# Batch norm's folded tables: the mean subtracted behind the products of tokens, tile sums and weights' loads moved into the attention, halves of groups

## The reference, cut to what matters

```python
h = _layernorm(x, axis=-1) * (1 + cb) + sb
q = jnp.einsum('bnd,de->bne', x, w_q)          # x is h here, 2048 columns
mean = jnp.mean(q, axis=(0, 1))
var = jnp.var(q, axis=(0, 1))
q = (q - mean) * jax.lax.rsqrt(var + BN_EPS) * bn_gamma + bn_beta
sim = jnp.einsum('pbnhd,hkpd->pbnhk', q, keys) # 16 groups of 32 keys
...                                            # top 8 of 8, experts, weighted sum
```

## Time and profile before

| | us |
|---|---|
| median of 3 runs (lowest to highest) | 2928.05 (2925.79 to 2930.73) |
| the profiled execution's own time | 2926.95 |
| its span, first to last instruction | 2925.2 |
| TensorE busy | 2720.0 (93%) |
| VectorE busy | 2235.5 (76%) |
| ScalarE busy | 2169.2 (74%) |
| GpSimd busy | 1780.2 (61%) |

### The profile page before, as it was taken

How to read it: one execution, slowest core, us unless ns; L and a number is a source line. 1 busy time by engine, 2 the same in 40 slices (tenths; PEclk the granted TensorE clock), 3 DMA queues, 4 the chain that set the end, 5 groups by cost and what they waited for, 6 DMA issues and landing times. The chain is left out here.

```text
span 2925.2 us, 77676 instructions
## 1 busy us (share of the span) xinstructions
PE 2720.0 (93%) x27972; PEld 2066.3 (71%) x27972; DVE 2235.5 (76%) x8496; ACT 2169.2 (74%) x4273; POOL 1780.2 (61%) x1788
## 2 busy tenths in 40 slices
PE   5999999999999999999999996599999999998588
PEld 3777777777777777777777775366767666766344
DVE  5566866776866776776767755699999999997585
ACT  3888888888888888888888882377767776776574
POOL 3788888888888888888888782234333433432121
PEclk9999999999999999999999997688878878878799
DMA  3000000000000000000000001100000000000000
GB/s 107 1 1 8 1 1 8 1 1 8 1 1 8 1 1 8 1 1 8 1 1 8 1 1 66 69 0 0 0 0 0 0 0 0 0 0 2 1 29 29
DMA packets 11793, 27.63 MB, mean 9 GB/s; under 512 B 1529, under 2 KB 6137, under 8 KB 11137
## 3 DMA queue, kind: packets, MB, share of 16 engines
q1 hardware_dynamic: 11618, 25.48, 2.5%
HBM read 17.07 MB, written 8.40 MB: 9 GB/s over the span
## 5 line engine op out<-in xcount | busy, mean ns | idle before, releaser
L284 POOL TENSOR_TENSOR probs_l<-probs,probs_h 128x512 fp32r<-128x512 f32 x1024 | 1302.7, 1294 | 302.0 <-ACT probs_h L378 297.3
L377 ACT ACTIVATE probs<-bank 128x512 f32<-128x512 f32 x1024 | 641.7, 627 | 266.6 <-PE bank L700 169.6
L539 DVE TENSOR_REDUCE maxes<-ring 128x1 f32<-128x512 f32 x1024 | 659.4, 686 | 181.3 <-PE ring L680 180.4
L378 ACT ACTIVATE probs_h<-bank 128x512 fp32r<-128x512 f32 x1024 | 644.1, 629 | 0.0
L699 PE MATMUL bank<-q_hh,k_hl 128*128 128x512 f32 x1024 | 424.4, 414 | 1.5 <-ACT probs_h L378 1.3
L700 PE MATMUL bank<-q_lm,k_h 65*128 65x512 f32 x1024 | 405.6, 396 | 0.0
L710 PE MATMUL obank<-probs_h,x_l 128*128 128x512 f32 x1024 | 404.7, 395 | 0.0
L712 PE MATMUL obank<-probs_h,x_h 128*128 128x512 f32 x1024 | 403.2, 394 | 0.0
L711 PE MATMUL obank<-probs_l,x_h 128*128 128x512 f32 x1024 | 402.6, 393 | 0.0
L680 PE MATMUL ring<-k_hl,q_hh 128*128 128x512 f32 x1024 | 339.6, 412 | 11.8 <-DVE maxes L539 7.2
L1085 ACT ACTIVATE low_hot<-obank 128x512 f16<-128x512 f32 x512 | 296.8, 604 | 55.3 <-PE obank L1264 42.1
(11 more groups left out here) (255 smaller groups left out, 4827.6 us busy)
## 6 DMA issues: line engine op xcount, KB each, us to landing
xt<-in_x SPq DMA_DIRECT2D x8, 512.0 KB, 10.1
out_x<-xt SPq DMA_DIRECT2D x8, 512.0 KB, 2.6
x<-out_x SPq DMA_DIRECT2D x1, 4096.0 KB, 12.2
out_x<-x SPq DMA_DIRECT2D x16, 256.0 KB, 2.0
mod<-out_x SPq DMA_DIRECT2D x3, 512.0 KB, 13.7
pk_wq<-in_w_q SPq DMA_DIRECT2D x1, 1024.0 KB, 6.1
pk_wqT<-in_w_qT SPq DMA_DIRECT2D x1, 1024.0 KB, 7.3
hot_rule<-in_hot_rule SPq DMA_DIRECT2D x1, 776.0 KB
```

The costliest lines, as they stand in the source:

```text
L284: nc.gpsimd.tensor_tensor(probs_l[:, i, :], probs[:, s % 4, :], probs_h[:, i, :].bitcast(F32), ALU.subtract).then_inc(low_ready, 1)
L377: nc.scalar.activation(probs[:, s % 4, :], st[s % 4], ACT.Exp)
L378: nc.scalar.activation(probs_h[:, i, :], st[s % 4], ACT.Exp).then_inc(st_free[s % 4], 1)
L539: nc.vector.tensor_reduce(maxes[:, i, k:k + 1], ring[bank_of(at)][:], AX.X, ALU.max).then_inc(rows_maxed, 1)
```

## The change

1. **Mean behind the products.** `xt` is no longer changed by the tables: TensorE adds up the products of the tiles as they are, and VectorE takes the outer product of the mean away from them (`outer`, then `cov` in one instruction). The experts subtract the mean where ScalarE copies the transposed tiles (`neg_mean` as bias of `hcT`), and the copy `pk_hT` loses its bias.
2. **Into the attention.** The tile sums of batches 0 to 6 (`tile_sums`, head 5, step 13, one batch later); the loads of the tables' weights, into tiles whose use is over (`spare`, `wmod_sb`), in SyncE's queue before the last batch's stores; the bias's product (`bias_terms` on GpSimd, then one matmul ahead of the last outputs); the products of the first 32 tiles, on TensorE behind its last outputs.
3. **Halves.** The last batch's norm goes by halves of four tiles (`last_moments`, `half_root`, `last_norm`), with a store each. The power, the scaled keys, the matmuls to `w_eff` and the copies go by halves of eight groups.
4. **Bias parts to GpSimd,** with two copies out by ScalarE ahead; `three_ones` too.
5. `hot_rule` gets 128 partitions; the added 31 are zero and never read.

```diff
-            for b in range(B):
+            for b in range(B - 1):
...
+            sp.wait_ge(x1_l_ready, TB * B)
+            for dst, src in table_loads:
+                sp.dma_start(dst, src).then_inc(table_loaded, 16)
+            for half in range(2):
+                tiles = slice((B - 1) * TB + 4 * half, (B - 1) * TB + 4 * half + 4)
+                sp.wait_ge(o_read, 6 * (B * H - 1) + 3 * half + 4)
+                sp.wait_ge(ring_o_read, 2 * (B * H - 1) + half + 2)
+                sp.dma_start(x_scratch[:, tiles, :], xt[:, tiles, :]).then_inc(last_stored[half], 16)
+            sp.wait_ge(table_loaded, 16 * len(table_loads))
...
+            def bias_terms():
+                pool.wait_ge(table_loaded, 16 * len(table_loads))
+                pool.wait_ge(w_ready, B * H + 1)
+                nc.gpsimd.sem_inc(turns, 1)
+                nc.gpsimd.tensor_tensor(bias_of, keysT, spread(scales[:, 1, :], 2, NK), ALU.mult).then_inc(bias_ready, 1)
...
-            root(2 * B)
+            bias_terms()
+            for half in range(2):
+                half_root(half)
...
+            def tile_sums(link, b):
+                dve.wait_ge(h2_ready, 2 * b + 2)
+                batch = xt[:, b * TB:(b + 1) * TB, :].rearrange("p t d -> p d t")
+                link(nc.vector.tensor_reduce((part_sum if b else tile_sum)[:], batch, AX.X, ALU.add))
+                if b:
+                    link(nc.vector.tensor_tensor(tile_sum[:], tile_sum[:], part_sum[:], ALU.add))
...
+                link(moments_of(B - 1, half))
+                for t in range(4 * half, 4 * half + 4):
+                    last = nc.vector.bn_aggr(mean_var[:, t], moments[:, t])
+                link(last)
+                nc.vector.tensor_scalar(var[:, four], mean_var[:, four, 1], LN_EPS, None, ALU.add).then_inc(var_ready, 1)
...
+                dve.wait_ge(rstd_ready, 2 * B + half)
+                link(normed(B - 1, half, centred))
+                link(nc.vector.tensor_tensor(centred[:, four], centred[:, four], spread(mod[:, 2, B - 1], 1, 4), ALU.mult))
+                dve.wait_ge(last_stored[half], 16)
+                nc.vector.tensor_tensor(xt[:, tiles], centred[:, four], spread(mod[:, 1, B - 1], 1, 4), ALU.add).then_inc(h2_ready, 1)
...
+                        if h == 5 and s == 13 and not first:
+                            tile_sums(link, b - 1)
...
-            for n in range(9):
-                second_norm(link, n, B - 1)
+                last_moments(link, half)
+            for half in range(2):
+                last_norm(link, half)
+            dve.wait_ge(h2_ready, 2 * B)
...
+            pe.wait_ge(bias_ready, 1)
+            pe.wait_ge(st_free[1], 4 * (B * H - 1) + 5)
+            nc.tensor.matmul(bank2[0][:, HALF:N], ones[:], bias_of.rearrange("p g k -> p (g k)"), start=True, stop=True)
             outputs(B - 1, H - 1, 1)
+            pe.wait_ge(st_free[2], 4 * (B * H - 1) + 5)
+            pe.wait_ge(h2_ready, B)
+            for i in range(TT // 2):
+                mm = nc.tensor.matmul(bank2[1][:, 0:D], xt[:, i, :], xt[:, i, :], start=(i == 0), stop=False)
+            mm.then_inc(tail_done, 1)
+            pe.wait_ge(tail_done, 1)
...
+            nc.scalar.activation(bias_sb[:], bias[0:96], ACT.Copy).then_inc(bias_out, 1)
+            nc.scalar.activation(sim_bias[:], bias[0:96], ACT.Copy).then_inc(bias_out, 1)
+            act.wait_ge(sum_done, 2)
+            nc.scalar.activation(neg_mean[:], banks[1][:, 0:1], ACT.Copy, scale=-1.0 / ntok).then_inc(mean_ready, 1)
...
+            pool.wait_ge(bias_out, 2)
+            nc.gpsimd.tensor_tensor(bias_left[:, 0], bias_sb[:], sim_bias[:], ALU.subtract).then_inc(bias_parts, 1)
...
+            for k in range(2):
+                groups = slice(HG * k, HG * k + HG)
+                pool.wait_ge(var_ready, k + 1)
+                nc.gpsimd.tensor_tensor(var[:, 2, groups], var[:, 1, groups], half_neg[:, 0:HG], ALU.pow).then_inc(rstd_ready, 1)
...
+            link(nc.vector.tensor_reduce(part_sum[:], h2[:, TT - TB:TT, :].rearrange("p t d -> p d t"), AX.X, ALU.add))
+            nc.vector.tensor_tensor(tile_sum[:], tile_sum[:], part_sum[:], ALU.add).then_inc(tile_sum_ready, 1)
...
+            link(nc.vector.tensor_scalar(outer[:], banks[0][:, 0:D], neg_mean[:], 1.0 / ntok, ALU.mult, ALU.mult))
...
+            nc.vector.scalar_tensor_tensor(cov[:], gram, 1.0 / ntok, outer[:], ALU.mult, ALU.add).then_inc(cov_ready, 1)
...
+                if k % 2:
+                    two = slice(4 * k - 4, 4 * k + 4)
+                    nc.vector.tensor_scalar(var[:, 1, two], var[:, 0, two], BN_EPS, None, ALU.add).then_inc(var_ready, 1)
+            for k in range(2):
+                groups = slice(HG * k, HG * k + HG)
+                dve.wait_ge(rstd_ready, k + 1)
+                link(nc.vector.tensor_tensor(var[:, 3, groups], var[:, 2, groups], scales[:, 0, groups], ALU.mult))
+                nc.vector.tensor_tensor(keys_s[:, groups], keysT[:, groups], spread(var[:, 3, groups], 2, NK), ALU.mult).then_inc(keys_ready, 1)
+            for k in range(2):
+                cols = slice(HG * NK * k, HG * NK * k + HG * NK)
+                dve.wait_ge(tables_done, k + 1)
+                link(nc.vector.tensor_copy(w_eff[:, cols], tables[k]))
...
+            for i in range(TT // 2, TT):
+                if i == TT - TB:
+                    pe.wait_ge(tile_sum_ready, 1)
+                    nc.tensor.matmul(banks[0][:, 0:D], ones[:], tile_sum[:], start=True, stop=True).then_inc(sum_done, 1)
+                    nc.tensor.matmul(banks[1][:, 0:1], tile_sum[:], ones[:, 0:1], start=True, stop=True).then_inc(sum_done, 1)
+                mm = nc.tensor.matmul(gram, h2[:, i, :], h2[:, i, :], start=False, stop=(i == TT - 1))
             mm.then_inc(gram_done, 1)
...
+            for k in range(2):
+                pe.wait_ge(keys_ready, k + 1)
+                for g in range(HG * k, HG * k + HG):
+                    mm = nc.tensor.matmul(tables[k][:, g % HG * NK:(g % HG + 1) * NK], spare[2 + k][:, g % HG, :], keys_s[:, g, :], start=True, stop=True)
+                mm.then_inc(tables_done, 1)
...
-                nc.scalar.activation(hcT[:], h_bank[:, 0:2 * P], ACT.Copy).then_inc(hcT_ready, 1)
+                nc.scalar.activation(hcT[:], h_bank[:, 0:2 * P], ACT.Identity, bias=neg_mean[:]).then_inc(hcT_ready, 1)
...
-                nc.scalar.activation(hT[:], h_bank[:, 0:2 * P], ACT.Identity, bias=mean_col[:]).then_inc(hT_ready, 1)
+                nc.scalar.activation(hT[:], h_bank[:, 0:2 * P], ACT.Copy).then_inc(hT_ready, 1)
...
-        mean_col = sb("mean_col", [P, 1])
+        neg_mean = sb("neg_mean", [P, 1])
+        tile_sum = sb("tile_sum", [P, D])
+        scales = sb("pk_scales", [P, 2, G])
+        spare = [sb(f"spare{i}", [P, 8, P]) for i in range(4)]
+        wmod_sb = sb("wmod_sb", [P, 6 * D])
+        table_loads = [(spare[i][:], args["w_q"][:, 8 * i:8 * i + 8, :]) for i in range(2)]
+        table_loads += [(spare[2 + i][:], args["w_qT"][:, 8 * i:8 * i + 8, :]) for i in range(2)]
+        table_loads += [(wmod_sb[:, 0:G * NK].rearrange("p (g k) -> p g k", g=G), args["keysT"]), (scales[:, 0, :], args["bn_gamma"]), (scales[:, 1, :], args["bn_beta"])]
...
-            hot_rule = ex("hot_rule", [CODES, SHARE * P], F16)
+            hot_rule = ex("hot_rule", [P, SHARE * P], F16)
```

133 lines of the change are left out of this document (59 added, 74 removed).

## The result

The changed kernel takes **2889.06 us** (median of 4 runs, 2884.44 to 2893.09) where the kernel before, run beside it, takes 2928.41 (2925.79 to 2930.73): a ratio of 0.9865, 95% interval 0.9847 to 0.9884. A second measurement of both gave 2887.92 against 2925.43 and the same ratio (0.9851 to 0.988). The profiled execution took 2891.28 us, its span is 2889.5, that is 35.7 less than before. The agreement is closer than the steps deserve: the norm and `cov` to `w_eff` gave 2.8 us more than forecast, because a wait that I had put into both is not there, and two pieces of 3 and 5 us that I had at nothing nearly cancel that.

The account below looks back on a forecast made before the run. The prediction took the table stage as one dependent chain, with the last batch's norm ahead of it, so whatever leaves it is won. Terms -1.8 - 30.9 - 1.9 + 0.1 = -34.5 us gave a median of 2893.5, range 2889 to 2900.

Parts of the forecast that it names:

- term 1: Last batch's norm in halves, up to the table block's first work: -1.8 us, or -2.7 without VectorE's wait.
- term 3: From `cov` to `w_eff`, in halves: 17.0 us instead of 18.94, -1.9; without the wait for GpSimd's power -3.4.
- the three items named for its low end: Range's low end: no GpSimd waits (-2.4), last matmuls partly fast (at most -3.5), runs differing 2.4 from their median.
- Term 2: Table block's first work to `cov`: 7.5 us instead of 38.45, -30.9, with sums and half the products off the chain.
- Terms at nothing: Head 5's tile sums, loads, `hot_rule` and barriers cost nothing; `hcT` hides in the experts' loop, +0.1 ahead of it.
- The loop did not feel `hcT`: Rival in the experts' loop: TensorE waits for `hcT` in each pair, 3.7 us in all: 2897; chance 0.06.
- `hot_rule` on one engine: Rival: `hot_rule`'s load stays at 27 GB/s, lands at 1829 and delays the experts: 2914; chance 0.05.
- The slower case: Tile sums priced by their 128 results, 13.8 us each in head 5 instead of 1.73: 2952; chance 0.03.
- The clock's rival: TensorE's clock falls at the table block's edge after 2.2 us of rest: +6 us, 2899.5; chance 0.09.

Follow-up runs that it names:

- the kernel with the subtraction: Changed kernel plus one unused GpSimd subtraction of 128x512 ahead of the second half's power in the last batch's norm; 2888.78 us (2887.73 to 2891.18).

## Why the prediction was right, and where it was wrong

**The mechanism held.** One dependent chain, and what leaves it is won: 36.7 us between the end of the heads and `w_eff`. What the prediction named for it is there: the clock at 1.00 up to `cov`, `hot_rule` before 1797, heads unchanged by the sums, the loop unchanged.

**What failed is a wait that does not exist.** The sum held 0.9 us in term 1 and 1.5 in term 3 for VectorE standing behind GpSimd's power; the runs show none (1.10 us beside a power and 1.11 without, 0.46 and 0.42). Without it the forecast would have been 2891.1, still 2.0 to 3.2 us above the two medians. The rest lies in what I had at nothing, the start of the program and of the experts. The range was too narrow by its own account too: 2893.5 less the three items named for its low end (2.4, 3.5 and 2.4) is 2885.2, and I wrote 2889; the 2887.92 of the second measurement lies between.

**Term 1, -1.8, was -2.84: the failed step is the wait.** I had half 1's power stop a normalizing instruction for 0.9 us, "since the slow case is the median". The slow rows were real, but GpSimd's work during the heads is its subtractions of 128x512, and the neighbour mattered: 1.10 us beside a power of 4 columns, 2.16 beside such a subtraction. The value without the wait, -2.7, was in the text. It was written as a bound; it should have been the forecast or at least half of it, since no row had a power as the cause.

**Term 2, -30.9, was -30.18: mis-sized.** `cov` took 8.27 us instead of 7.5. I divided a window of 4 us by its 38 instructions, but a window counts those that reach over its edges too: in the row of the last 8 products 16 instructions take 2.03 us. With 0.113 (5.43 us for 48) the 24 products take 5.43 instead of 5.05. The tile sum took 1.96 (1.73 forecast), with slack. The clock held, but not for my reason: the rest was 0.99 us and not 2.2, because the halves of the norm were faster and the first 32 products, which ran 7.31 us from 1773.67, longer. Behind a rest of 2.04, in the kernel with the subtraction, it fell: I had given that rival 0.09 at a rest of about the length at which it came true there. But I had its price wrong as well, 6 us for the products all slow; there the clock was back at 1.00 by 1788, and it cost 1.6.

**Term 3, -1.9, was -3.65: the same failed step.** The scaling of the first keys took 0.46 us beside the second power. The bound without the wait, -3.4, was right to 0.25 us, of which TensorE's last matmuls make 0.16 (6.87 instead of 7.03 us). Their clock is partly luck: the same kernel again took 6.17 us for them, and the term was -4.35.

**Terms at nothing** held in the attention and in the loop. Seven sums cost 2.02 us each and an addition of 0.70, and in head 5 VectorE still rests 4.05 us where it rested 6.70.

**Two pieces were missing.** The 3 us at the start could not be read from the profile of before. The 5 us at the experts' start could at least have been looked for: VectorE's comparison and GpSimd's copy start 0.07 us apart in the old trace, and GpSimd's instruction behind that copy takes 4.39 us where its like before it took 0.41. Whatever moves the stage ahead, or its clock, throws that die again. That the sum came out near is luck: +5.0 and -3.0 met -2.8 from the waits that were not there.

**The rivals.** The loop did not feel `hcT`. `hot_rule` on one engine would have cost 15.6, with the start's 2.5 of the trace in it (2903.5; I had 2914 with another stage around it). The slower case has no support: 1.96 to 2.03 us a sum. The clock's rival was closer than its chance said.

## What to carry to other kernels

Before a wait for a shared resource goes into a sum, ask which operation, of which size, the slow rows stood beside; if the new neighbour is another one, take both values as open and forecast by the row without the wait. When an early part gets faster, look in the trace of before for pairs of instructions on two engines that start within a few tenths of a microsecond of each other and of which one makes the other wait: such a race can turn and give back the gain, and a wait of 0.4 us on the one that can afford it holds the order. And work that is moved under the end of another stage may be worth more than its length if it keeps TensorE's clock up over the barrier, here 8.9 us for 7.2.

## What the runs showed of the hardware that I had not expected

- GpSimd's power on 128x4 and 128x8 (1.03 and 1.64 us) leaves VectorE's instructions at 1.10 us for four and 0.46 for a scaling; its subtraction on 128x512 doubles the four to 2.16. The other way round, a copy of 32x128 on GpSimd takes 0.28 us ahead of VectorE's comparison and 4.44 behind it.
- TensorE kept its granted clock of 1.00 over a rest of 0.99 us and lost it 0.5 us after the end of one of 2.04. The length alone does not decide: around a rest of 3.30 us in eight traces it fell between 2.4 us into the rest and 1.3 us behind it.
- 31 more rows in an array in DRAM that is not read until 1.7 ms later, and the gates' broadcast load at the program's start took 19.5 to 20.3 us in the three traces in which I read it, against 22.8 in the kernel before and 22.6 with 97 rows.
